# First attention of a hybrid layer: key features computed once, stored in HBM and loaded again

## The reference, cut to what matters

```python
def _softmax_kernel_feats(data, proj, is_query):
    data_dash = jnp.einsum('bnhd,md->bnhm', data * dn, proj)
    diag = jnp.sum(jnp.square(data), axis=-1, keepdims=True) * (dn * dn) / 2.0
    mx = jnp.max(data_dash, axis=-1, keepdims=True) if is_query else jnp.max(data_dash)
    return ratio * (jnp.exp(data_dash - diag - mx) + EPS_KERN)
...
kf = _softmax_kernel_feats(k, proj, False)
kv = jnp.einsum('bnhm,bnhd->bhmd', kf, v)
num = jnp.einsum('bnhm,bhmd->bnhd', qf, kv)
den = jnp.einsum('bnhm,bhm->bnh', qf, jnp.sum(kf, axis=1))
attn_out = jnp.einsum('bnhd,hdo->bno', num / den[..., None], Wo)
out1 = _layernorm(x + attn_out, ln1_g, ln1_b)
h = jax.nn.elu(out1 @ W1 + b1)
return _layernorm(out1 + h @ W2 + b2, ln2_g, ln2_b)
```

## Time and profile before

| | before |
|---|---|
| median of 3 runs | 2456.73 us |
| profiled execution | 2462.02 us, span 2459.9 us |
| PE busy | 1858.3 us (76%) |
| DVE busy | 1640.3 us (67%) |
| POOL busy | 1261.6 us (51%) |
| ACT busy | 1106.3 us (45%) |
| key maximum | 0 to 83.5 us |
| attention blocks 0, 1, 2, 3 start at | 83.3, 213.5, 405.1, 601.9 us |
| last feed-forward | 794.3 to 830.5 us |

### The profile page before, as it was taken

How to read it: one execution, slowest core, us unless ns; L and a number is a source line. 1 busy time by engine, 2 the same in 40 slices (tenths; PEclk the granted TensorE clock), 3 DMA queues, 4 the chain that set the end, 5 groups by cost and what they waited for, 6 DMA issues and landing times. The chain is left out here.

```text
span 2459.9 us, 45628 instructions
## 1 busy us (share of the span) xinstructions
PE 1858.3 (76%) x15915; PEld 1074.0 (44%) x15915; DVE 1640.3 (67%) x4684; ACT 1106.3 (45%) x2069; POOL 1261.6 (51%) x1244
## 2 busy tenths in 40 slices
PE   8998888877888678782989988988898778784000
PEld 3556446445555556561334443434343346563000
DVE  8357577578568665385888888887888365375322
ACT  1363544545445446561357644544454546663000
POOL 0153146656657676675246530342153467577776
PEclk9999989989989879896689987898898979997555
DMA  9400000100100688783314221203121288785222
GB/s 370 174 1 5 1 1 24 35 16 18 35 22 31 249 294 263 240 280 118 78 52 115 60 65 39 63 31 89 29 84 51 104 295 271 250 274 180 61 60 56
DMA packets 134252, 275.69 MB, mean 112 GB/s; under 512 B 29644, under 2 KB 44620, under 8 KB 128124
## 3 DMA queue, kind: packets, MB, share of 16 engines
q1 hardware_dynamic: 101256, 205.60, 25.4%
q0 software_dynamic: 32768, 67.17, 9.3%
HBM read 146.34 MB, written 125.93 MB: 111 GB/s over the span
## 5 line engine op out<-in xcount | busy, mean ns | idle before, releaser
L1504 POOL DMA_INDIRECT slots_in<-g_xs,g_place x512 | 508.6, 993 | 298.8 <-ACT b_pT L2595 145.9
L2595 ACT ACTIVATE b_pT<-b_psE 128x512 f32<-128x512 f32 (+3 forms) x768 | 331.8, 492 | 374.4 <-PE b_psE L2496 206.7
L1531 POOL DMA_INDIRECT r_xs<-slots_out,g_place x336 | 328.3, 977 | 228.4 <-issue 86.2
L2347 DVE TENSOR_REDUCE b_peak<-b_psM 128x1 f32<-128x512 f32 (+3 forms) x768 | 387.9, 549 | 78.1 <-PE b_psM L2479 45.4
L2476 PE MATMUL b_psM<-b_stacks 72*128 72x512 bf16 (+3 forms) x768 | 260.1, 376 | 56.7 <-DVE b_peak L2347 24.7
L2492 PE MATMUL b_psE<-b_stacks 75*128 75x512 bf16 (+3 forms) x768 | 235.6, 361 | 14.7 <-ACT b_pT L2595 12.9
L1531 POOL DMA_INDIRECT g_xs<-slots_out,g_place x176 | 173.9, 988 | 93.4 <-issue 50.9
L2506 PE MATMUL b_psV<-b_pT,b_vb 128*32 128x512 f32 (+3 forms) x1536 | 180.4, 552 | 4.0 <-ACT b_ctxu L2602 3.7
L2476 PEld LDWEIGHTS b_psM<-b_stacks 72*128 72x128 bf16 x768 | 79.5, 105 | 224.9 <-DVE b_peak L2347 133.9
L2112 DVE COPY m_staged_w<-wgd 128x192 f32 x512 | 108.1, 281 | 86.2 <-PE m_psY L1817 75.2
L2112 DVE COPY n_staged_w<-wgd 128x192 f32 x512 | 106.1, 277 | 83.3 <-PE n_psY L1817 47.1
(11 more groups left out here) (664 smaller groups left out, 4068.3 us busy)
## 6 DMA issues: line engine op xcount, KB each, us to landing
wgd<-in_w_gdT SPq DMA_DIRECT2D x20, 1536.0 KB, 10.5
slots_in<-g_xs SPq DMA_DIRECT2D x26, 1024.0 KB
m_rows<-slots_in SPq DMA_DIRECT2D x104, 256.0 KB
slots_out<-m_y SPq DMA_DIRECT2D x104, 256.0 KB
n_rows<-slots_in SPq DMA_DIRECT2D x104, 256.0 KB
slots_out<-n_y SPq DMA_DIRECT2D x104, 256.0 KB
b_stacks<-q_parts SPq DMA_DIRECT2D x48, 192.0 KB
b_stacks<-k_parts SPq DMA_DIRECT2D x48, 192.0 KB
```

The costliest lines, as they stand in the source:

```text
L1504: self.nc.gpsimd.indirect_dma_start(self.G.slots_in[self.h], bass.IndirectOffsetOnAxis(self.G.place[:, TPH * self.h + t, k:k + 1], 0), sel ...
L1531: self.nc.gpsimd.indirect_dma_start(self.rows(i)[:, k, :], None, self.G.slots_out[t // TPH], bass.IndirectOffsetOnAxis(self.G.place[:, t, ...
L2347: nc.vector.reduce_max(to, taking()[:, 0:size], AX.X).then_inc(m_taken, 1)
L2595: nc.scalar.activation(pT[:, e % KEPT, h, q0:HALF], psE[:, j % BANKS, q0:HALF], ACT.Exp, scale=SCALE).then_inc(e_taken, 1)
```

## The change

In the key maximum the product's operands are swapped, so that a product is one tile of tokens with all 1024 features of it. ACT copies it from PSUM to a ring of four tiles in SBUF; DVE takes the maximum there, and SP stores the tile to a new tensor `key_dash` in HBM (32 stores of 512 KB). Eight of the 26 zero fills stay between the stores, eight go into the key loop of block 0, ten after it. In the key loops the features are no longer computed: SP loads each tile into the ring of arguments once the exponential two tiles back has read it, and DVE subtracts in place. The order on PE becomes keys, key-value products of tile t-2, values half 0, values half 1, with the values in two banks; on ACT the square comes first. In the feed-forward DVE adds the two parts of the activation, and PE multiplies the sum once.

```diff
--- before.py
+++ after.py
...
-def attn_a_weights(nc, m):
+def attn_a_weights(nc, m, G):
...
+    fills = iter([slots.rearrange("(n p j) d -> n p (j d)", n=ZERO_FILLS, p=P)[n] for slots in G.slots_in for n in range(ZERO_FILLS)])
+
+    def fill_zeros(sp, count):
+        for fill in itertools.islice(fills, count):
+            sp.dma_start(fill, G.zeros[:]).then_inc(A.zero_fills, 16)
+
+    A.fill_zeros = fill_zeros
...
     RING_F = 3
+    KEPT_F = 4
...
-        pmax = m1.sbuf("pmax", [P, BATCH, PAIRS])
+        pmax = m1.sbuf("pmax", [P, BATCH, TPB])
+        dashes = m1.sbuf("dashes", [P, KEPT_F, HD])
+        kept, copied = [m1.sem(f"kept{i}") for i in range(KEPT_F)], m1.sem("copied")
...
             sp.wait_ge(zeros_made, 1)
-            for slots in G.slots_in:
-                fill = slots.rearrange("(n p j) d -> n p (j d)", n=ZERO_FILLS, p=P)
-                for n in range(ZERO_FILLS):
-                    sp.dma_start(fill[n], G.zeros[:]).then_inc(zero_fills, 16)
+            for n in range(TILES):
+                sp.wait_ge(copied, n + 1)
+                sp.dma_start(G.key_dash[n], dashes[:, n % KEPT_F, :]).then_inc(kept[n % KEPT_F], 16)
+                if n % 4 == 3:
+                    A.fill_zeros(sp, 1)
+            for k in kept:
+                sp.wait_ge(k, 16 * TILES // KEPT_F)
             sp.wait_ge(landed, 64)
...
             def features(b):
-                pe.wait_ge(xnT_ready, 2 * b + 2)
-                for c in range(PAIRS):
-                    n = PAIRS * b + c
+                for t in range(TPB):
+                    n = TPB * b + t
+                    if t % 4 == 0:
+                        pe.wait_ge(xnT_ready, 2 * b + t // 4 + 1)
                     if n >= RING_F:
-                        pe.wait_ge(taken, n - RING_F + 1)
+                        pe.wait_ge(copied, n - RING_F + 1)
                     else:
                         pe.wait_ge(folded, 1)
                     for u in range(2):
-                        last = nc.tensor.matmul(psF[:, n % RING_F, u, :], wkp[:, c, :], G.xnT[:, b, u * HALF:(u + 1) * HALF], start=True, stop=True)
+                        last = nc.tensor.matmul(psF[:, n % RING_F, u, :], G.xnT[:, b, t * P:(t + 1) * P],
+                                                wkp[:, 4 * u:4 * u + 4, :].rearrange("p c m -> p (c m)"), start=True, stop=True)
                     last.then_inc(feats, 1)
-                    if b + 1 < BATCH and c in TURNS_AT:
-                        turn(b + 1, TURNS_AT.index(c))
+                    if b + 1 < BATCH and t in TURNS_AT:
+                        turn(b + 1, TURNS_AT.index(t))
...
-            pe.wait_ge(taken, PAIRS * BATCH - 1)
+            pe.wait_ge(copied, TILES)
...
-            for b in range(BATCH):
-                for u in range(2):
-                    act.wait_ge(x_turned, 2 * b + u + 1)
-                    nc.scalar.activation(G.xnT[:, b, u * HALF:(u + 1) * HALF], psT[:, u, :], ACT.Copy).then_inc(xnT_ready, 1)
+            def take_turned(b, u):
+                act.wait_ge(x_turned, 2 * b + u + 1)
+                nc.scalar.activation(G.xnT[:, b, u * HALF:(u + 1) * HALF], psT[:, u, :], ACT.Copy).then_inc(xnT_ready, 1)
+
+            for u in range(2):
+                take_turned(0, u)
+            for n in range(TILES):
+                b, t = divmod(n, TPB)
+                act.wait_ge(feats, n + 1)
+                if n >= KEPT_F:
+                    act.wait_ge(kept[n % KEPT_F], 16 * (n // KEPT_F))
+                    act.wait_ge(taken, n - KEPT_F + 1)
+                nc.scalar.activation(dashes[:, n % KEPT_F, :], psF[:, n % RING_F, :, :].rearrange(both), ACT.Copy).then_inc(copied, 1)
+                if b + 1 < BATCH and t in TURNS_AT:
+                    take_turned(b + 1, TURNS_AT.index(t))
...
             def peaks(b):
-                for c in range(PAIRS):
-                    n = PAIRS * b + c
+                for t in range(TPB):
+                    n = TPB * b + t
                     next(pieces, None)
-                    dve.wait_ge(feats, n + 1)
-                    nc.vector.reduce_max(pmax[:, b, c:c + 1], psF[:, n % RING_F, :, :].rearrange(both), AX.X).then_inc(taken, 1)
+                    dve.wait_ge(copied, n + 1)
+                    nc.vector.reduce_max(pmax[:, b, t:t + 1], dashes[:, n % KEPT_F, :], AX.X).then_inc(taken, 1)
...
             def key_square_sums(t):
                 dve.wait_ge(k_halved, t + 1)
+                nc.vector.drain()
                 nc.vector.reduce_sum(shift[:], fold2[:, t % 2, :, :], AX.X).then_inc(k_diag, 1)
                 nc.vector.drain()

             def key_argument(t):
-                dve.wait_ge(kd_done, t + 1)
-                if t >= 2:
-                    dve.wait_ge(k_exp, t - 1)
-                nc.vector.tensor_tensor(arg[:, t % 2, :].rearrange(heads, k=MF), dash, bc(shift[:], MF), ALU.subtract).then_inc(k_arg, 1)
+                dve.wait_ge(kd_landed[t % 2], 16 * (t // 2 + 1))
+                argument = arg[:, t % 2, :].rearrange(heads, k=MF)
+                nc.vector.tensor_tensor(argument, argument, bc(shift[:], MF), ALU.subtract).then_inc(k_arg, 1)
...
         @block.sync
         def _(sp):
+            for t in range(TPB):
+                if t >= 2:
+                    sp.wait_ge(k_exp, t - 1)
+                sp.dma_start(arg[:, t % 2, :], G.key_dash[TPB * b + t]).then_inc(kd_landed[t % 2], 16)
+                if b == 0:
+                    A.fill_zeros(sp, 1)
+                elif t == 1:
+                    routing_loads(sp, W, R)
             if b == 0:
+                A.fill_zeros(sp, HALVES * ZERO_FILLS)
                 sp.wait_ge(zero_fills, 16 * HALVES * ZERO_FILLS)
             else:
-                routing_loads(sp, W, R)
                 sp.wait_ge(R.router_landed, 64)
...
-            def key_dash(t):
+            def values(t, u):
                 if t >= 1:
-                    pe.wait_ge(k_arg, t)
-                for u in range(2):
-                    last = nc.tensor.matmul(psB[:, u, :], xT[:, t * P:(t + 1) * P], wkp[:, 4 * u:4 * u + 4, :].rearrange("p c m -> p (c m)"),
-                                            start=True, stop=True)
-                last.then_inc(kd_done, 1)
-
-            def values(t, u):
-                if t + u >= 1:
-                    pe.wait_ge(v_ready, 2 * t + u)
-                nc.tensor.matmul(psB[:, 2, :], xT[:, t * P:(t + 1) * P], wv[:, u * HALF:(u + 1) * HALF],
+                    pe.wait_ge(v_ready, 2 * t + u - 1)
+                nc.tensor.matmul(psB[:, u, :], xT[:, t * P:(t + 1) * P], wv[:, u * HALF:(u + 1) * HALF],
                                  start=True, stop=True).then_inc(v_done, 1)
...
                 else:
-                    pe.wait_ge(k_arg, TPB)
+                    pe.wait_ge(v_ready, 2 * TPB)
...
             for t in range(TPB):
                 fill(t, 0)
-                if t:
-                    values(t, 0)
+                key(t)
                 fill(t, 1)
-                key(t)
+                if t >= 2:
+                    if t == 2 and b:
+                        pe.wait_ge(B.sums_taken, 2)
+                    add_kv(t - 2, range(HA // 2))
                 fill(t, 2)
-                if t:
-                    values(t, 1)
+                if t >= 2:
+                    add_kv(t - 2, range(HA // 2, HA))
                 fill(t, 3)
-                key_dash(t)
+                values(t, 0)
                 fill(t, 4)
-                if t:
-                    if t == 1 and b:
-                        pe.wait_ge(B.sums_taken, 2)
-                    add_kv(t - 1, range(HA // 2))
-                    fill(t, 5)
-                    add_kv(t - 1, range(HA // 2, HA))
-                else:
-                    values(0, 0)
-                    fill(t, 5)
-                    values(0, 1)
+                values(t, 1)
+                fill(t, 5)
                 fill(t, 6)
             fill(TPB, 0)
             query(0)
+            add_kv(TPB - 2, range(HA))
             query_dash(0)
             add_kv(TPB - 1, range(HA))
...
-                nc.scalar.activation(v[:, t % 2, 8 * u:8 * u + 8, 0:DH], psB[:, 2, :].rearrange(heads, k=DH), ACT.Copy).then_inc(v_ready, 1)
+                nc.scalar.activation(v[:, t % 2, 8 * u:8 * u + 8, 0:DH], psB[:, u, :].rearrange(heads, k=DH), ACT.Copy).then_inc(v_ready, 1)
...
             for t in range(TPB):
+                take(t, 0)
+                square_keys(t)
+                take(t, 1)
                 if t:
                     key_exponentials(t - 1)
-                take(t, 0)
-                if t:
-                    take_values(t, 0)
-                take(t, 1)
-                square_keys(t)
                 take(t, 2)
                 if t:
                     key_features(t - 1)
                 sigmoids(t, 0)
-                if t == 0:
-                    take_values(t, 0)
+                take(t, 3)
+                take_values(t, 0)
+                take(t, 4)
```

(19 more changed lines are left out.)

11 lines of the change are left out of this document (6 added, 5 removed).

## The result

The changed kernel takes 2445.6 us against 2458.9 (medians of 20 runs each); the ratio is 0.9948 [0.9933, 0.9964]. The gain is 13 us, where 46 were forecast (2411, range 2397 to 2434): the sign was right, the size was not. A second set of runs gave 0.9928 [0.9900, 0.9956]: 18 us by the ratio, 12 by the medians. One execution of this study, of run 2 (2916 us at a mean clock of 0.54), belongs to a slow state of the chip and is in no ratio. The profiled execution took 2448.3 us around a span of 2445.9, 14.0 less than before.

The account below looks back on a forecast made before the run. PE was taken to bound block 0, PE and DVE the key maximum, a mix blocks 1 to 3. Gains 2 + 16 + 25.5 + 2.5 = 46 took the profiled 2462.0 to 2416, median 2411 us; range 2397 to 2434.

Parts of the forecast that it names:

- part 4: Key loops of blocks 1 to 3: earlier keys and less PE work gain 8.5 us per block, 25.5 in all.
- Part 1: Key maximum: PE no longer waits for DVE's maximum, DMA is late next; gain 2 us, bounds gain 5, loss 9.
- rival (d): Key maximum: DMA writes at 358 GB/s, first stage ends 8.5 us later; gain 35.5, 2421 us; chance 0.06.
- Part 2: Block 0: feature product leaves PE's loop, 5.38 us per tile instead of 7.10; gain 16 us, bounds 12 and 18.
- Part 3: Feed-forward in blocks 1 to 3: fewer PE products; 2.6 us gained on DVE, 7.1 on PE.
- The first half: Block 1's key loop up to argument 3: a walk through the durations puts it 8 us ahead, at 269 to 270.
- The second half: Block 1's key loop after argument 3: DVE's own work bounds to argument 6, no further gain; then 3 us for ranks.
- The 3 for the ranks: Late key loop: ranks lose the feature product and half a tile's key-value products ahead; 3 us more, 11 at vector copy.
- Rival (a): Routing hides it: DVE bounds blocks 1 to 3 throughout, gaining 3.7 us each; 31.5 in all, 2425 us; chance 0.17.
- The clock: Key loops of blocks 1 to 3: two more PE stalls at the lower clock, 1.3 us each; minus 2.5 per block.
- The contention: Key loops of blocks 1 to 3: arguments with two SBUF operands held up beside POOL; 0.5 us per block.
- Part 5: Last feed-forward: DVE's first add goes at 810.7 instead of 813.24, then DVE bounds to the end; gain 2.5 us.

Follow-up runs that it names:

- run 2: Changed kernel with the feed-forward's summing taken out (two products per chunk, minimum on one tensor): ratio to the kernel before 0.9930 [0.9903, 0.9958].
- the second pair: A second profile each of the kernel before and the unaltered changed kernel; the changed kernel's ratio in that set of runs was 0.9928 [0.9900, 0.9956].
- Run 4: Changed kernel with all 26 zero fills issued in block 0, none between the stores: ratio to the kernel before 0.9892 [0.9866, 0.9917].
- run 6: Changed kernel with the rectifier's result left in PSUM instead of SBUF: ratio to the kernel before 0.9928 [0.9902, 0.9955].
- Run 5: Changed kernel with keys and squares made one tile earlier still, two tiles ahead: ratio to the kernel before 0.9918 [0.9888, 0.9947].
- Runs 13 and 14: Changed kernel, all zero fills in block 0, keys and squares two tiles ahead, sigmoids earlier; without, then with 11 extra PE products per block: ratios 0.9840 and 0.9815.
- Run 7: Changed kernel with 23 extra unread products per block in PE's stalls of blocks 1 to 3: ratio to the kernel before 0.9900 [0.9876, 0.9924].
- Run 11: Kernel before with 30 unread products added at the start of block 0, to start later: ratio 1.0108 [1.0067, 1.0148].

## Why the prediction was too large

The forecast was 46 for the whole. In the first pair of profiles the parts below make -0.7 + 15.1 + 6.3 - 0.4, 20 us, before the experts, and 6 are lost behind them: 14. Of the 32 that are missing, 19 are in part 4.

*Part 1, key maximum: gain 2, measured a loss of 0.7 (0.2 in the second pair).* The mechanism was the one named, DMA as what is late next; its price was taken from the fills alone (425 GB/s). Stores and fills together ran at 402 to 414, 62 us for 25.2 MB instead of 59. This was rival (d)'s direction, at a quarter of its price. Run 4 shows that the eight fills held the stage.

*Part 2, block 0: gain 16, measured 15.1 (16.2 at the vector copy; 11.6 in the second pair, whose kernel before was 3.2 us shorter there).* Right: where PE runs without a gap, taking work from it gave its whole time back.

*Part 3, feed-forward: 2.6 on DVE and 7.1 on PE at the start of the loops.* Right as positions. But the operation that it buys them with stands in SBUF with both operands, and I priced it by the quiet 0.69; at argument 1, where 3.7 were forecast, DVE was 2.0 ahead in block 1 and in blocks 2 and 3 had lost nearly all again (47.2 and 47.8 us after the start, for 47.8 and 47.7). That the new operation's own blocking does this is not shown: in run 6, where it is gone, argument 1 stands at 48.8 and 48.7.

*Part 4, key loops of blocks 1 to 3: 25.5, measured 6.3 (3.1, 3.5 and -0.3) and 3.1 in the second pair.* This is the step that failed. The prediction walked to argument 3 ("I reach it at 269 to 270, 8 ahead") and went on: "Then DVE's own work bounds to argument 6: nothing more", with 3 more for the ranks.

The first half was too short. In block 1 argument 3 came 3.9 ahead. Of the missing 4, 1.7 were lost before argument 1; from there the way over exponential 1, the turns, the scores and tile 3 took 14.9 us (16.8 before) where the walk has some 12.5, and on it PE ran at the half clock, keys 3 at 3.62 us for 1.88.

The second half was wrong in kind, and this weighs more: it is a wait that the prediction left out. DVE's work did not bound to argument 4. That argument stands behind MAX8 in DVE's order, and MAX8 waits for the routing's sigmoid, 26.1 us after argument 1's end (27.6 before) with or without the feature products in PE's way. Run 5 shows it: with argument 3 at 52.5, 11.5 ahead of the kernel before and so more than the 8 forecast, DVE idled 8.6 us at MAX8, which came no earlier. The 3 for the ranks came as 0.8 (argument 6 was 2.0 ahead, argument 7 2.8). Runs 13 and 14 gave 16 to 22 us in these blocks over the changed kernel once both chains were shortened, 23 and 28 over the first profile of the kernel before: the room that I counted was there, but in another order than the change's.

Rival (a), 11 us for the three blocks, came nearer, and its headline, routing hides it, was right. Its mechanism was not: it has DVE busy throughout, and the rows show DVE idle 10.9 us ahead of sum 3 and 2.7 ahead of MAX8. Not even its 11 were reached.

The clock was in the sum with 2.5 us per block. Run 7 gives 3.3 us back in block 2, 1.2 to 3.1 in block 3 and nothing in block 1: about right in size.

The contention was in it with 0.5 us per block, for the arguments alone. They took 1.21 us on the mean in blocks 1 and 3, and in block 2 one of the eight took 2.12: right in size. What was missed are the others: the two-tensor operation, and the small products pushed beside POOL's. The Trainium skill's rule (SBUF — State Buffer, "SBUF: two separate sides") is borne out by the 1.78 us of a 128x4 product more exactly than by the earlier trace rows: such an operation ends when POOL's ends.

*Part 5, last feed-forward: 2.5, measured -0.4 (0.5 in the second pair).* DVE's add came 2.65 us earlier, as said. "From there DVE bounds to the end" failed in the first profile: POOL, which issues 18 sends there, went from 17.8 to 20.5 us for them (991 to 1139 ns each) and ended 33.8 us after the stage's start instead of 30.6; DVE ended at 33.8 too (35.4), and the next stage came 2.8 us after both. In the second profile DVE did bound, but two of its new operations took 2.33 and 1.76 us, and it ended at 35.0. Both are the contention of part 3; with the rectifier's result in PSUM (run 6) the stage lasted 35.0 us for 36.2.

*Outside the sum: 0 forecast, 6.2 lost in the first pair and 17.1 in the second.* The second attention was 7.5 to 12 us longer in both profiles of the changed kernel than in both of the kernel before. Run 11 shows that the old code can run the longer way too; whether the moment or chance decides stays open.
